# Four pairs of maximum units in each head group of the last attention, reduced as b and a - b with ScalarE and VectorE sharing them

## The reference

```python
qh = (q @ Wq + bq).reshape(B, LQ, HEADS, D_K).transpose(0, 2, 1, 3)     # B 4, LQ 512, 16 heads of 16
kh = (k @ Wk + bk).reshape(B, LKV, HEADS, D_K).transpose(0, 2, 1, 3)    # LKV 1601
scores = jnp.einsum('bhqd,bhkd->bhqk', qh, kh) * scale
attn = jax.nn.softmax(scores, axis=-1)
out = jnp.einsum('bhqk,bhkd->bhqd', attn, vh)
```

## Time and profile before

| what | value |
|---|---|
| median of 3 runs | 1461.89 us (1460.13 to 1464.0) |
| time of the profiled execution | 1463.16 us |
| span of the profiled execution | 1461.2 us |
| TensorE busy, share of the span | 93% |
| VectorE busy | 72% |
| ScalarE busy | 53% |
| steady stretch of the last attention | 904 to 1318 us |

### The profile page before, as it was taken

One profiled execution on the slowest core, in us unless ns is written; L12 is line 12 of the kernel. 1 busy time (PEld: TensorE's weight loads), 2 busy tenths in 40 slices (PEclk: granted clock), 3 DMA queues, 4 the chain that ended last, 5 costly groups with the idle time before them and its releaser, 6 DMA issues. The chain is left out here.

```text
span 1461.2 us, 24901 instructions
## 1 busy us (share of the span) xinstructions
PE 1358.8 (93%) x9358; PEld 757.9 (52%) x9358; DVE 1055.0 (72%) x2359; ACT 773.2 (53%) x1066; POOL 318.4 (22%) x409
## 2 busy tenths in 40 slices
PE   7997999899999989769988799999999999999996
PEld 3665688748989977423336323333333333333385
DVE  5897466551222248869966879999999999997177
ACT  2443566511111102346673226888788888888754
POOL 2111422350000037643436340000000000000011
PEclk9999999999999999969999859999999999999999
DMA  9665633367888822864413531322323432220001
GB/s 334 222 206 189 212 133 122 119 238 243 282 299 271 304 64 85 268 195 135 125 36 103 197 107 49 88 68 69 68 69 88 99 85 69 68 69 1 1 1 58
DMA packets 152841, 198.68 MB, mean 136 GB/s; under 512 B 15723, under 2 KB 124799, under 8 KB 152594
## 3 DMA queue, kind: packets, MB, share of 16 engines
q1 hardware_dynamic: 141004, 165.34, 36.4%
q0 software_dynamic: 9200, 29.64, 6.5%
q10 hardware_dynamic: 2518, 2.13, 0.5%
HBM read 136.08 MB, written 60.70 MB: 135 GB/s over the span
## 5 line engine op out<-in xcount | busy, mean ns | idle before, releaser
L2422 DVE TENSOR_REDUCE xa_part<-psum 128x1 f32<-128x512 f32 (+1 forms) x768 | 462.6, 661 | 20.3 <-PE psum L2273 18.5
L2373 ACT ACTIVATE xa_P<-psum 128x1024 f32<-128x1024 f32 (+1 forms) x416 | 403.4, 1020 | 105.2 <-PE psum L2297 104.7
L2297 PE MATMUL psum<-sa_Q,xa_K 48*128 48x512 bf16 (+3 forms) x1664 | 268.1, 382 | 3.9 <-DMA sa_Q<-xa_mrow 2.9
L2273 PE MATMUL psum<-xa_K,sa_Q 48*128 48x512 bf16 (+1 forms) x768 | 239.3, 388 | 4.9 <-DVE xa_part L2422 1.5
L2313 PE MATMUL psum<-xa_P,xa_V 128*32 128x512 f32 (+1 forms) x1664 | 223.5, 609 | 0.4 <-ACT xa_P L2373 0.4
L2273 PEld LDWEIGHTS psum<-xa_K,sa_Q 48*128 48x128 bf16 x768 | 59.3, 94 | 232.1 <-DVE xa_part L2422 160.6
L2297 PEld LDWEIGHTS psum<-sa_Q,xa_K 48*128 48x128 bf16 (+3 forms) x1664 | 105.8, 97 | 69.4 <-ACT xa_P L2373 21.0
L2419 DVE CUSTOM_DVE_ANT_0 psum<-psum,cf_sb 128x512 f32<-128x512 f32 (+1 forms) x240 | 111.4, 518 | 17.5 <-PE psum L2273 17.2
L1550 PEld LDWEIGHTS psum<-xtT,wgu 128*128 128x128 f32 x992 | 115.5, 192 | 5.8 <-issue 4.6
L1550 PE MATMUL psum<-xtT,wgu 128*128 128x128 f32 x992 | 115.9, 275 | 1.4 <-issue 0.8
L2373 ACT ACTIVATE sa_P<-psum 128x1024 f32<-128x1024 f32 (+3 forms) x128 | 83.4, 702 | 48.2 <-PE psum L2297 48.2
(11 more groups left out here) (270 smaller groups left out, 2126.5 us busy)
## 6 DMA issues: line engine op xcount, KB each, us to landing
wgu<-in_f_gu SPq DMA_DIRECT2D x31, 1024.0 KB, 6.1
xa_K<-kx SPq DMA_DIRECT2D x192, 100.1 KB, 4.7
wdn<-in_f_dn SPq DMA_DIRECT2D x31, 512.0 KB, 6.4
vx<-xv_v SPq DMA_DIRECT2D x48, 256.0 KB, 2.8
xa_V<-vx POOLq DMA_DIRECT2D x16, 768.0 KB, 6.3
sa_Q<-qs SPq DMA_DIRECT2D x64, 96.0 KB, 2.4
sa_K<-ks SPq DMA_DIRECT2D x64, 96.0 KB, 2.4
sa_Q<-qx SPq DMA_DIRECT2D x64, 96.0 KB, 2.3
```

The costliest lines, as they stand in the source:

```text
L2273: last = pe.matmul(out[:, 0:width], hb.q(u)[tile:tile + HALF, to, qt * P:(qt + 1) * P], hb.k(u)[tile:tile + HALF, to, cut[e]:cut[e] + widt ...
L2297: last = pe.matmul(out(j), hb.k(u)[tile:tile + depth, to, kt * P:kt * P + r], hb.q(u)[tile:tile + depth, to, q0(kt):L], start=(half == 0), ...
L2373: act.activation(Pr[0:r, (u * KT + kt) % PR, h:h + 2, 0:w_], S_PS(p)[0:r, :, 0:w_], ACT.Exp, scale=SCALE).then_inc(s_exp, 1)
L2422: dve.tensor_reduce(part[:, g % 2, col + qt, e:e + 1], src[:, 0:cut[e + 1] - cut[e]], AX, ALU.max).then_inc(s_1free, 1)
```

## The change

Of each group's units, four pairs are formed: pieces e = 0 and e = 1 (call them a and b) of one head and query tile. Unit n = 13, 29, 37 and 45 (`ABOVE`) of a group from group 1 on now computes a - b in PSUM: a matmul with the queries and keys 0 to 511, and one that accumulates on it, with the negated queries `Qn` and keys 512 to 1023. Unit n + 2 (`UNDER`) computes b, as before. ScalarE takes max(a - b, 0) of the first into `excess` (in SBUF), VectorE adds it to b and takes the maximum of the sum, in one instruction with its read out. VectorE doesn't touch the first unit of a pair. GpSimd negates the queries of each group (`negated`, 48 partitions by 1024 elements), in its queue ahead of `parts`. The bank of an `ABOVE` unit is free when ScalarE is done with it. `Qn` and `excess` lie in `xT`, so their tile's name in rows is xT_sb. Group 0 has the same order of units, but reduces all of them as before. The order of the other units moves a little (`paired_units`), and `part` has a fifth column.

```diff
+PAIRED = {3: (1, 0), 7: (3, 0), 9: (3, 1), 11: (3, 2)}
+def paired_units(cuts):
+    taken = [(h, qt, e) for h, qt in PAIRED.values() for e in range(2)]
...
+        if four in PAIRED and turn % 2:
+            units.append(PAIRED[four] + (turn // 2,))
+            continue
...
+    ABOVE = () if causal else [4 * four + 1 for four in sorted(PAIRED)]
+    UNDER = () if causal else [n + 2 for n in ABOVE]
...
+                def negated(g):
+                    u = g % R
+                    if g >= 2:
+                        pool.wait_ge(s_mh, g - 1)
+                    pool.wait_ge(hb.s_kq[u], 16 * hb.LOADS * (g // R + 1))
+                    pool.tensor_scalar(Qn[ROW_TILE:ROW_TILE + HALF, u], hb.q(u)[ROW_TILE:ROW_TILE + HALF, 0:G // 2, :], -1.0, None,
+                                       ALU.mult).then_inc(s_neg, 1)
...
                 if not causal:
+                    negated(1)
                     parts(0)
...
+                        if g + 1 < GROUPS:
+                            negated(g + 1)
                         parts(g)
...
                     if place >= R1 and place - R1 in by_scalar:
                         pe.wait_ge(s_mrow, by_scalar[place - R1] + 1)
+                    elif place >= R1 and place - R1 in by_relu:
+                        pe.wait_ge(s_excess, by_relu[place - R1] + 1)
...
+                    elif paired(g, n, ABOVE):
+                        pe.wait_ge(s_neg, g)
+                        pe.matmul(out[:, 0:BANK], hb.q(u)[tile:tile + HALF, to, qt * P:(qt + 1) * P],
+                                  hb.k(u)[tile:tile + HALF, to, 0:BANK], start=True, stop=False, tile_position=(tile, 0))
+                        last = pe.matmul(out[:, 0:BANK], Qn[tile:tile + HALF, u, to, qt * P:(qt + 1) * P],
+                                         hb.k(u)[tile:tile + HALF, to, BANK:2 * BANK], start=False, stop=True,
+                                         tile_position=(tile, 0))
...
+                def above(g, n):
+                    i = pair_of(g, n)
+                    act.wait_ge(s_1, at(g, n) + 1)
...
+                    act.activation(excess[:, i % 2, :], bank(at(g, n)), ACT.Relu).then_inc(s_excess, 1)
+
                 def group(g, u, before):
...
                         if kt == 0 and before:
                             output(g - 1)
+                        for a, n in [unit for turn in range(TURNS) for unit in here[kt * TURNS + turn]]:
+                            if paired(g + a, n, ABOVE):
+                                above(g + a, n)
...
+                    if paired(g, n, ABOVE):
+                        return
                     dve.wait_ge(s_1, at(g, n) + 1)
...
+                    if paired(g, n, UNDER):
+                        i = pair_of(g, n)
+                        dve.wait_ge(s_excess, i + 1)
+                        dve.tensor_tensor_reduce(src, src, excess[:, i % 2, :], 1.0, LOWEST, ALU.add, ALU.max,
+                                                 part[:, g % 2, col + qt, e:e + 1]).then_inc(s_1free, 1)
```

More of the change, by code:

```diff
@@ L2001 @@
 LEFT = 128
+LOWEST = -3e38
 def units_of_cuts(cuts):
@@ L2010, in units_of_cuts @@
         four, turn = divmod(n, 4)
+        odd = (0, four % 2, (four + 1) % 2, 1)[turn]
+        heads = (odd, odd + 2, 1 - odd, 3 - odd)
+        kinds = (short, long) if turn == 1 else (long, short)
+        found = [kind[h] for half in (heads[:2], heads[2:]) for kind in kinds for h in half if kind[h]]
+        units.append(found[0].pop(0))
+    return units
+PAIRED = {3: (1, 0), 7: (3, 0), 9: (3, 1), 11: (3, 2)}
+def paired_units(cuts):
+    taken = [(h, qt, e) for h, qt in PAIRED.values() for e in range(2)]
+    long = {h: [u for u in [(h, qt, e) for qt in range(TB) for e in range(cuts - 2)] if u not in taken] + [(h, None, cuts - 1)]
+            for h in range(G)}
+    short = {h: [(h, qt, cuts - 2) for qt in range(TB)] for h in range(G)}
+    units = []
+    for n in range(G * (TB * (cuts - 1) + 1)):
+        four, turn = divmod(n, 4)
+        if four in PAIRED and turn % 2:
+            units.append(PAIRED[four] + (turn // 2,))
+            continue
         odd = (0, four % 2, (four + 1) % 2, 1)[turn]
@@ L2073, in heads_loop @@
     else:
-        units = units_of_cuts(CUTS)
+        units = paired_units(CUTS)
     U = len(units)
+    ABOVE = () if causal else [4 * four + 1 for four in sorted(PAIRED)]
+    UNDER = () if causal else [n + 2 for n in ABOVE]
+    paired = lambda g, n, of: g >= 1 and n in of
     R1 = UNIT_BANKS
@@ L2102, in heads_loop, with maxima_at @@
     by_scalar = {} if causal else {shift_at(g): g for g in range(GROUPS)}
+    pair_of = lambda g, n: (g - 1) * len(ABOVE) + (ABOVE if n in ABOVE else UNDER).index(n)
+    by_relu = {at(g, n): pair_of(g, n) for g in range(1, GROUPS) for n in ABOVE}
     def reduced(place):
-        return place + 1 - sum(at_ <= place for at_ in by_scalar)
+        return place + 1 - sum(at_ <= place for at_ in by_scalar) - sum(at_ <= place for at_ in by_relu)
+    def maxima_at(before, ahead):
+        after = [(1, n) for n in range(EARLY, U)] * (ahead >= 1) + [(2, n) for n in range(EARLY)] * (ahead >= 2)
+        if not before:
+            after = [(1, n) for n in range(LEAD, EARLY)] + after
+        ends = [min(len(after), due(point, U if before else len(after))) for point in range(POINTS)]
+        return [after[ends[point - 1] if point else 0:ends[point]] for point in range(POINTS)]
     COLS = G * TB
@@ L2115, in heads_loop @@
         Pr = sb(name + "_P", [P, PR, G, L], F32)
-        part = sb(name + "_part", [P, 2, COLS, CUTS], F32)
+        part = sb(name + "_part", [P, 2, COLS, CUTS if causal else CUTS + 1], F32)
+        if not causal:
+            Qn = env.xT[:, 0, 0:R * G // 2 * L // 2].bitcast(BF16).rearrange("p (u h n) -> p u h n", u=R, h=G // 2)
+            excess = env.xT[:, 1, 0:2 * BANK].rearrange("p (u n) -> p u n", u=2)
+            s_lowest = sem(name + "_lowest")
+            s_neg = sem(name + "_neg")
+            s_excess = sem(name + "_excess")
         mx = hb.mx
@@ L2212, in _ @@
                 if not causal:
+                    pool.memset(part[:, :, :, :].rearrange("p a c e -> p (a c e)"), LOWEST).then_inc(s_lowest, 1)
                     for n in LATER:
@@ L2217, in _ @@
                     load_v(g, g)
+                def negated(g):
[5 more added lines that the diff above has]
+                                       ALU.mult).then_inc(s_neg, 1)
+                    pool.wait_ge(s_neg, g)
                 def parts(g):
@@ L2318, in group @@
                 def group(g, u, first, before, ahead):
[L2320 to L2323, removed]
+                    here = maxima_at(before, ahead)
                     for kt in range(KT):
@@ L2334, in group @@
                                 values(g - 1, (u + R - 1) % R, KT - 1, None)
-                            while done < min(len(after), due(point, U if before else len(after))):
-                                a, m = after[done]
+                            for a, m in here[point]:
                                 unit(g + a, (u + a) % R, m, first + (u + a) // R)
-                                done += 1
                                 if (a, m) == (2, BEHIND):
@@ L2363, in output @@
                     act.activation(OT[:, g:g + 1, :].rearrange("p g n -> p (g n)"), O_PS, ACT.Copy).then_inc(s_ot, 1)
+                def above(g, n):
+                    i = pair_of(g, n)
+                    act.wait_ge(s_1, at(g, n) + 1)
+                    if i >= 2:
+                        g_, n_ = (i - 2) // len(UNDER) + 1, UNDER[(i - 2) % len(UNDER)]
+                        act.wait_ge(s_1free, reduced(at(g_, n_)))
+                    act.activation(excess[:, i % 2, :], bank(at(g, n)), ACT.Relu).then_inc(s_excess, 1)
                 def group(g, u, before):
+                    here = maxima_at(before, min(2, GROUPS - 1 - g))
                     for kt in range(KT):
@@ L2413, in unit @@
                     col = h % 2 * COLS // 2 + h // 2 * TB
-                    if qt is None:
+                    if paired(g, n, UNDER):
[3 more added lines that the diff above has]
+                                                 part[:, g % 2, col + qt, e:e + 1]).then_inc(s_1free, 1)
+                    elif not causal and not g and n in ABOVE:
+                        dve.tensor_reduce(part[:, 0, col + qt, CUTS:CUTS + 1], src, AX, ALU.max).then_inc(s_1free, 1)
+                    elif qt is None:
                         dve.tensor_reduce(part[:, g % 2, col:col + TB, e], src[:, 0:TB * LEFT].rearrange("p (t k) -> p t k", t=TB),
@@ L2427, in of_cuts @@
                         dve.wait_ge(s_mh, g - 1)
-                    dve.tensor_reduce(mx[:, g % 2, :], part[:, g % 2, :, :], AX, ALU.max, negate=True).then_inc(s_cuts, 1)
+                    columns = CUTS if g else CUTS + 1
+                    dve.tensor_reduce(mx[:, g % 2, :], part[:, g % 2, :, 0:columns], AX, ALU.max, negate=True).then_inc(s_cuts, 1)
```

(2 more changed lines are left out.)

## The result

The changed kernel takes 1473.38 us (median of 6 runs, 1468.49 to 1474.67), the one before 1462.39 us (6 runs, 1460.13 to 1464.0). The ratio is 1.007, with a 95% interval of 1.0054 to 1.0085: 11.0 us slower between the medians, where 12.1 us were forecast.

What follows compares the result with a forecast made beforehand. TensorE, streaming without a gap at 2.41 us a key tile, was taken as the bound. 12.1 (TensorE) + 1.7 (chain) - 1.7 (group 0's loop) = +12.1 us, so 1474.0 us; range 1460 to 1482, likeliest case 1468 to 1482.

Steps and rivals of the forecast that it cites:

- Step 1: VectorE: a pair loses a reduce of 0.60, its add and maximum takes 0.05 more; net 0.55, worth nothing under TensorE's pace.
- Step 2: TensorE, steady stretch: second matmul of a - b starts 0.22 later, the other half idles; 55 x 0.22 = 12.1 us.
- Step 3: Steady stretch, chain of a - b, relu, sum: ends meet within 0.05 us; loss 0.03 a pair, 1.7 us.
- Step 4: Group 0's loop, where VectorE runs back to back: five pairs there give -1.7 us together, bounds -2.7 and +1.
- Step 5: GpSimd's negation of the queries: at most 2.8 us, ends 7 us ahead of `parts`; cost nothing.
- Step 6: Order of the other units, fifth column, one fill of `part`: no more than 0.3 us in all, both ways; 0.

Runs made afterwards that it cites:

- the first experiment: The changed kernel with the first unit of a pair as one matmul, without the negated second one; 1459.99 us, ratio 0.9991 to the kernel before.

## Why the prediction was right

**What bounds the kernel: right, and shown.** The pace counted from starts said TensorE, 1.98 + 2 x 0.22, against busy shares and the table of waits. VectorE relieved by 25 us changed nothing in the steady stretch, a matmul more cost its slot.

**Step 1, VectorE:** right. The add and maximum is followed after 0.62 us, where I took 0.65, and the relief turned into waits.

**Step 2, TensorE, 55 x 0.22 = 12.1 us:** the size was right, 12.2 us between the two `values` that bracket the units. Its reason held only in part. I wrote that the even head's unit would be held back by the queue and its half of the array idle for the slot. It was not: it starts ahead of the second matmul. The cost is there because the odd half's row of matmuls is then seven long, and both halves must end before `values`. The repeats on both halves show it. That the two mechanisms give the same number here is luck.

**Step 3, the chain, 1.7 us:** the ends meet as worked out, but without loss. Key tiles with a pair took 2.62, which is 2.41 and the slot, so the 0.03 a pair put on top were not there. A relu 0.5 later cost 0.47 a tile.

**Step 4, group 0's loop, -1.7 us:** mis-sized. At full clock it was -0.8. A tile of it went from 3.1 to 3.4 us: a relu stands there behind an exponential (882.13 to 882.74), and the third unit after its a - b waits 0.25 us for the bank and starts at 882.79. Four other tiles gained 0.15 to 0.4. The profiled execution gained 1.7 us more in the two key tiles ahead of them, where the clock came back sooner, which no step had.

**Step 5, the negation:** right: 2.78 us, at the upper bound of 2.8, and 6.5 and 4.7 us ahead of its deadline in two groups, where I had 7.

**Step 6, the order at 0:** right for the change and wrong as a statement about the order. It costs 0.08 us a place, 0.34 a group, once VectorE empties the bank, as pairs for group 1 alone showed; the relu on ScalarE hides it.

**The sum:** +12.1 forecast; +11.4 in the trace without the clock's part, +11.0 between medians. Steps 3 and 4 were off by 1.7 and 0.9 in opposite directions, so part of the closeness is luck.

## What to carry to other kernels

When two engines both show 98% busy, count the distance from start to start of each engine's instructions and add up what each needs for a repeating piece; the one whose sum gives the observed length is the bound. Long waits of weight loads for another engine are not a sign that this engine is late, as long as the matmuls' starts have no hole. A change that moves work off one engine and puts a little on another pays with the little, if the other is the bound: here four slots of 0.22 us a group bought 2.3 us of idle VectorE (33.6 less 5.9 us of waits, over the 12.2 groups from 900 to 1300).

## What the runs showed of the hardware

Matmuls on the two halves of the array's rows start independently, to the extent of one instruction at least: a unit for the even half started at 1076.29 while the second matmul for the odd half, ahead of it in the program, started at 1076.51. The even half's unit is first in 42 of the 60 pairs of this trace. Eight more matmuls, four on each half, cost as much as four on one: key tiles of 2.70 us both times.

The completions count in the program's order all the same. The record of that even unit's matmul ends at 1076.68, but the trace's semaphore events have the counter of finished units go up at 1076.90 and again 0.03 later, both after the second matmul of a - b (1076.89) and none before. So it is at all 42 places; an ordinary unit is counted 0.015 us after its modelled end. ScalarE is free at 1076.73 and its relu starts at 1076.92; VectorE's reduce of the even unit starts at 1076.96.

Three banks that go round make a loop of their own. A long unit right behind `values` that VectorE reduces needs 0.39 for its matmul and 0.69 for the reduce before the third unit after it may be written, and in the kernel with pairs for group 1 alone that made a key tile 2.48 for 2.41. With a short unit there (0.36 and 0.62, before), or with ScalarE emptying the bank in 0.60 (the first experiment), it was 2.41.
